# Cross attention 0 of a Perceiver kernel: key and value projections as three products of float16 halves, and x loaded first

## The reference

```python
def _mha_cross(x, mem, in_w, in_b, out_w, out_b):
    wq, wk, wv = (in_w[:D], in_w[D:2 * D], in_w[2 * D:])
    q = _split_heads(x @ wq.T + bq, H)
    k = _split_heads(mem @ wk.T + bk, H)
    v = _split_heads(mem @ wv.T + bv, H)
    scores = jnp.einsum('bhqd,bhkd->bhqk', q, k) * (1.0 / math.sqrt(hd))
    attn = jax.nn.softmax(scores, axis=-1)
    out = _merge_heads(jnp.einsum('bhqk,bhkd->bhqd', attn, v))
    return out @ out_w.T + out_b
x_self = _prob_sparse_self_attn(x, self_out_w, self_out_b)
x = _layernorm(x + x_self, ln1_g, ln1_b)
x_cross = _mha_cross(x, memory, cross_in_w, cross_in_b, cross_out_w, cross_out_b)
```

## Time and profile before

| what | value |
|---|---|
| time, median of 3 runs (all) | 3562.58 us (3560.48 to 3575.97) |
| the profiled execution | 3577.74 us, its span 3576.0 us |
| busy over the span | PE 93%, PEld 67%, DVE 70%, ACT 53%, POOL 31% |
| mean granted clock of TensorE | 0.958 of full speed |
| first instruction of TensorE | 23.0 us |
| cross attention 0 | 188.5 to about 1121 us |
| in it, from 300 to 1000 us: DVE's waits for maxima (L977) | 131.6 us |
| ACT's waits for scores (L998) there | 237.5 us |
| POOL's waits for evicted keys (L1173) and for queries (L1079) there | 327.6 and 100.7 us |
| 24 spread_keys DMAs on SP's queue, one batch | issued from 599.25 to 615.51 us, each landing 2.2 us after its issue |

### The profile page before, as it was taken

The page is one execution under the profiler, slowest core; times in us unless marked ns, Lnnn a source line. Parts: engine busy times, 40 slices in busy tenths (PEclk is TensorE's granted clock), DMA queues, the critical chain, the costliest instruction groups (busy, mean ns, idle before and its releaser), DMA issues. The chain is left out here.

```text
span 3576.0 us, 83011 instructions
## 1 busy us (share of the span) xinstructions
PE 3337.8 (93%) x32677; PEld 2384.9 (67%) x32913; DVE 2495.1 (70%) x7178; ACT 1909.3 (53%) x2964; POOL 1102.4 (31%) x795
## 2 busy tenths in 40 slices
PE   6879999999998888899999999999999999797999
PEld 4746666666666666677777777777777777565666
DVE  5657777777775444677777777777777777566544
ACT  4326666566665232566666666666666666444333
POOL 1033334333341001544434433444344333130000
PEclk9969999999999779999999999999999999897999
DMA  1023333333320010111111111111111110100000
GB/s 53 2 68 76 75 82 71 74 76 76 81 62 16 2 48 22 42 43 43 33 31 42 43 34 31 43 43 37 34 37 43 34 33 19 48 1 27 1 1 13
DMA packets 95125, 146.45 MB, mean 41 GB/s; under 512 B 14960, under 2 KB 72336, under 8 KB 93968
## 3 DMA queue, kind: packets, MB, share of 16 engines
q1 hardware_dynamic: 94736, 141.12, 14.7%
HBM read 100.66 MB, written 1.05 MB: 28 GB/s over the span
## 5 line engine op out<-in xcount | busy, mean ns | idle before, releaser
L2252 DVE SCALAR_TENSOR_TENSOR arena<-banks,arena 128x512 f16<-128x512 f32 (+1 forms) x1024 | 554.3, 583 | 308.7 <-ACT arena L2341 307.4
L2341 ACT ACTIVATE arena<-banks 128x512 f16<-128x512 f32 (+1 forms) x1024 | 471.3, 512 | 400.2 <-PE banks L2159 397.1
L1092 DVE TENSOR_REDUCE arena<-banks 128x1 f32<-128x512 f32 (+1 forms) x896 | 529.4, 627 | 186.7 <-PE banks L977 181.5
L1189 ACT ACTIVATE arena<-banks 128x1024 f32<-128x1024 f32 (+1 forms) x448 | 425.1, 964 | 315.3 <-PE banks L998 312.5
L2264 DVE CUSTOM_DVE_ANT_0 arena<-banks,arena 128x1024 f32<-128x1024 f32 (+1 forms) x512 | 494.3, 987 | 32.1 <-issue 31.9
L2348 ACT ACTIVATE arena<-arena 128x1601 f32<-128x1601 f32 x256 | 417.7, 1632 | 107.7 <-DVE arena L2270 105.7
L2159 PE MATMUL banks<-consts,arena 128*128 128x128 f32 (+1 forms) x3328 | 456.8, 275 | 7.1 <-DVE arena L2252 7.0
L2173 PE MATMUL banks<-arena 128*128 128x256 f16 (+1 forms) x1664 | 456.1, 274 | 0.7 <-ACT arena L2355 0.7
L2175 PE MATMUL banks<-arena 128*128 128x256 f16 (+1 forms) x1664 | 451.3, 271 | 0.0
L2174 PE MATMUL banks<-arena 128*128 128x256 f16 (+1 forms) x1664 | 450.3, 271 | 0.0
L2159 PEld LDWEIGHTS banks<-consts,arena 128*128 128x128 f32 (+1 forms) x3328 | 364.9, 141 | 17.2 <-issue 10.0
(11 more groups left out here) (360 smaller groups left out, 6141.2 us busy)
## 6 DMA issues: line engine op xcount, KB each, us to landing
arena<-in_ctxT SPq DMA_DIRECT2D x64, 800.5 KB, 4.5
arena<-arena SPq DMA_DIRECT2D x768, 50.0 KB, 2.2
arena<-in_ctx SPq DMA_DIRECT2D x32, 768.0 KB
arena<-in_mask SPq DMA_DIRECT2D x32, 200.1 KB, 4.6
arena<-in_m2w SPq DMA_DIRECT2D x3, 2048.0 KB, 8.3
arena<-in_xw SPq DMA_DIRECT2D x1, 2048.0 KB, 11.8
weights<-in_weights SPq DMA_DIRECT2D x1, 1920.0 KB, 7.8
arena<-in_ctx SPq DMA_DIRECT2D x32, 32.5 KB
```

The costliest lines, as they stand in the source:

```text
L1092: eng.tensor_reduce(o, s, AX, ALU.max).then_inc(a_max, 1)
L1189: eng.activation(pr[0:w, at % 4, :].rearrange("p (x n) -> p x n", x=2)[:, :, 0:n], c.ps[0:w, bank:bank + 2, 0:n], ACT.Exp, scale=scale).th ...
L2252: eng.scalar_tensor_tensor(out=part(ptl, g, gr), in0=turned(gr), scalar=TOP, in1=part(pth, g, gr), op0=ALU.mult, op1=ALU.subtract).then_in ...
L2341: eng.activation(part(pth, g, gr), turned(gr), ACT.Copy, scale=TOP).then_inc(t_high, 1)
```

## The change

- Context and the two weight matrices of the key and value projections are scaled into float16's range and split into a high and a low float16 half; each projection is the sum of three products (high x high, high x low, low x high). The first pair (i = 0) keeps the float32 projections.
- For the weights this is done once: `weights_peaks` and `weights_split` on VectorE, with `weights_row` on TensorE between them (a matmul with ones, through bank 7).
- For each further batch: `magnitudes` on ScalarE sums the absolute values of each context row of 1601 (128 partitions) after exps 5 of even units, `diagonal` on GpSimd spreads the sums on a diagonal, `ctx_row` on TensorE adds them over partitions (bank 7, after mix 6 of odd units), `ctx_scale` on VectorE makes the scale (reduce, floor, reciprocal, unit) after queries, and `split_ctx` on GpSimd scales and splits the context (three instructions, 128 x 1601) after split_queries. For batch (1, 0) ctx_row and ctx_scale stand in step 4 of the first unit, and magnitudes after its exps 0.
- The evictions of keys and values get a scale from memory; context loads wait for the split of the batch before in place of the projections.
- The loads are x in two halves, then consts, rows, weights, with semaphores of their own; the statistics and the normalisation of x alternate by group.

```diff
     def sp(eng):
+        x = A["x"].rearrange("(i b) l d -> (b l) i d", b=2)
+        eng.dma_start(c.x[:, 0:G, :], x[:, 0:G, :]).then_inc(c.x_loaded[0], 16)
+        eng.dma_start(c.x[:, G:PAIRS, :], x[:, G:PAIRS, :]).then_inc(c.x_loaded[1], 16)
+        eng.dma_start(c.c[:], A["consts"]).then_inc(c.consts_loaded, 16)
+        eng.dma_start(c.r[:], A["rows"]).then_inc(c.loaded, 16)
         eng.dma_start(c.w[:], A["weights"]).then_inc(c.loaded, 16)
-        eng.dma_start(c.r[:], A["rows"]).then_inc(c.loaded, 16)
-        eng.dma_start(c.c[:], A["consts"]).then_inc(c.loaded, 16)
-        eng.dma_start(c.x[:], A["x"].rearrange("(i b) l d -> (b l) i d", b=2)).then_inc(c.loaded, 16)
...
-    m.after = [(c.loaded, 64), (constant, 5)]
+    m.after = [(constant, 5)]
...
-        norms.dve_stats(eng, lambda i: c.x[:, i, :])
-        for g in range(GROUPS):
-            norms.dve_apply(eng, g, lambda i: c.x[:, i, :], lambda i: xn[:, i, :])
+        for g in range(GROUPS + 1):
+            if g < GROUPS:
+                if g < 2:
+                    eng.wait_ge(c.x_loaded[g], 16)
+                norms.dve_measure(eng, g, lambda i: c.x[:, i, :])
+            if g > 0:
+                norms.dve_apply(eng, g - 1, lambda i: c.x[:, i, :], lambda i: xn[:, i, :])
...
         def body(i, more):
-            if more:
-                load_ctx(i + 1, 0)
+            if i == 0 and more:
+                load_ctx(1, 0)
+            if i > 0 and more:
+                load_ctx(i + 1, 1)
             spread_keys(i, 1, 0)
             spread_keys(i, 1, 1)
+            if i == 0 and more:
+                load_ctx(1, 1)
+            if i + 2 < PAIRS:
+                load_ctx(i + 2, 0)
             if more:
-                load_ctx(i + 1, 1)
                 spread_keys(i + 1, 0, 0)
                 spread_keys(i + 1, 0, 1)
...
+        def diagonal(i, b):
+            n = batch_no(i, b)
+            eng.wait_ge(c_total, n + 1)
+            wait_if(eng, c_row, n)
+            eng.tensor_tensor(diag_c, c.C("ident"), total[:, b, :].to_broadcast([P, P]), ALU.mult).then_inc(c_diag, 1)
+
+        def split_ctx(i, b):
+            n = batch_no(i, b)
+            x = ctxT[:, b, :]
+            eng.wait_ge(c_inverse, n + 1)
+            eng.tensor_tensor(x, x, per_c[:, b, :].to_broadcast([P, S]), ALU.mult).then_inc(c_scaled, 1)
+            eng.wait_ge(c_scaled, n + 1)
+            if i > 1:
+                eng.wait_ge(v_ps, (i - 1) * 8 + 4 * b + 4)
+            eng.tensor_tensor(ch[:, b, 0:S], x, c.one[:].to_broadcast([P, S]), ALU.mult).then_inc(c_high, 1)
+            eng.wait_ge(c_high, n + 1)
+            eng.tensor_tensor(cl[:, b, 0:S], x, ch[:, b, 0:S], ALU.subtract).then_inc(c_split, 1)
...
         def body(i, more):
             if more:
-                for b in range(2):
-                    split_keys(i + 1, b)
-                    split_queries(i + 1, b)
+                split_keys(i + 1, 0)
+                diagonal(i + 1, 1)
+                split_queries(i + 1, 0)
+                split_ctx(i + 1, 1)
+                split_keys(i + 1, 1)
+                if i + 2 < PAIRS:
+                    diagonal(i + 2, 0)
+                split_queries(i + 1, 1)
+                if i + 2 < PAIRS:
+                    split_ctx(i + 2, 0)
...
+            eng.matmul(o, wh[:, 0, :], ch[:, b, a:z], start=True, stop=False)
+            eng.matmul(o, wh[:, 0, :], cl[:, b, a:z], start=False, stop=False)
+            eng.matmul(o, wl[:, 0, :], ch[:, b, a:z], start=False, stop=True).then_inc(k_ps, 1)
...
+                    eng.matmul(o, ch[:, b, r], wh[:, 1, :], start=True, stop=False)
+                    eng.matmul(o, ch[:, b, r], wl[:, 1, :], start=False, stop=False)
+                    mm = eng.matmul(o, cl[:, b, r], wh[:, 1, :], start=False, stop=True)
...
+        def ctx_row(i, b):
+            n = batch_no(i, b)
+            take_bank7((c_top, n + 1))
+            eng.wait_ge(c_diag, n + 1)
+            eng.matmul(c.ps[:, 7, 2 * P:3 * P], ones, diag_c, start=True, stop=True).then_inc(c_row, 1)
...
+                        elif more:
+                            ctx_row(1, 0)
                     elif st == 6 and v % 2 == 1 and more:
                         queries(i + 1, v // 2)
                     mix(i, v, st)
+                    if st == 6 and v == 1 and more:
+                        ctx_row(i + 1, 1)
+                    if st == 6 and v == 3 and i + 2 < PAIRS:
+                        ctx_row(i + 2, 0)
...
+        def ctx_scale(i, b):
+            n = batch_no(i, b)
+            eng.wait_ge(c_row, n + 1)
+            eng.tensor_reduce(top_c, c.ps[:, 7, 2 * P:3 * P], AX, ALU.max).then_inc(c_top, 1)
+            eng.wait_ge(c_top, n + 1)
+            eng.tensor_scalar(floor_c, top_c, 1e-25, 1 / TOP, ALU.max, ALU.mult).then_inc(c_floor, 1)
+            eng.wait_ge(c_floor, n + 1)
+            eng.reciprocal(per_c[:, b, :], floor_c).then_inc(c_inverse, 1)
+            if i > 1:
+                eng.wait_ge(v_made, (i - 1) * 8 + 4 * b + 4)
+            eng.tensor_scalar(units[:, b, :], per_top, floor_c[:, 0:1], None, ALU.mult).then_inc(c_units, 1)
...
+            eng.activation(o, ps, ACT.Identity, bias=c.W("c_bk"), scale=units[:, b, 0:1]).then_inc(k_copied, 1)
...
+                eng.activation(o, s, ACT.Identity, scale=units[0:w, b, 1:2]).then_inc(v_made, 1)
+
+        def magnitudes(i, b):
+
+            eng.wait_ge(ctx_loaded[b], i * 16 + 16)
+            if i > 1:
+                eng.wait_ge(v_ps, (i - 1) * 8 + 4 * b + 4)
+                eng.wait_ge(c_diag, batch_no(i - 1, b) + 1)
+            eng.activation(ch[:, b, 0:S], ctxT[:, b, :], ACT.Abs, accum_out=total[:, b, :]).then_inc(c_total, 1)
```

More of the change, by code:

```diff
@@ L808, in cross_attention_0 @@
     om, s1, rd = k.f32(4, L), k.f32(L), k.f32(L)
-    sem = lambda n: c.sem(f"x0_{n}")
+    ch, cl = k.f16(2, S + 1), k.f16(2, S + 1)
+    wh, wl = k.f16(2, D), k.f16(2, D)
+    ones, diag_w, diag_c = k.f32(P), k.f32(2, P), k.f32(P)
+    peak_w, top_w, per_top, to_f16 = (k.f32(2) for _ in range(4))
+    total, top_c, floor_c, per_c = k.f32(2, 1), k.f32(1), k.f32(1), k.f32(2, 1)
+    units = k.f32(2, 2)
+    TOP = 32768.0
+    sem = lambda n: c.sem(f"x0_{n}")
+    ones_set, w_peaks, w_diag, w_row, w_top, w_floor, w_inverse, w_high, w_low = (sem(f"w_{n}") for n in (
+        "ones", "peaks", "diag", "row_psum", "top", "floored", "inverse", "high", "low"))
+    c_total, c_diag, c_row, c_top, c_floor, c_inverse, c_units = (sem(f"ctx_{n}") for n in (
+        "total", "diag", "row_psum", "top", "floored", "inverse", "units"))
+    c_scaled, c_high, c_split = sem("ctx_scaled"), sem("ctx_high"), sem("ctx_split")
     two = lambda n: [sem(f"{n}{i}") for i in range(2)]
@@ L907, in pool @@
         split_queries(0, 1)
+        if PAIRS > 1:
+            diagonal(1, 0)
+            split_ctx(1, 0)
         def body(i, more):
             if more:
-                for b in range(2):
-                    split_keys(i + 1, b)
-                    split_queries(i + 1, b)
+                split_keys(i + 1, 0)
[8 more added lines that the diff above has]
+                    split_ctx(i + 2, 0)
         pairs(eng, body)
@@ L927, in keys @@
             take_bank7((k_copied, i * 8 + 4 * b + n + 1))
[L928 to L931 removed]
+            a, z = chunks[n]
+            o = c.ps[:, 7, 0:z - a]
+            if i == 0:
+                if n == 0:
+                    eng.wait_ge(ctx_loaded[b], 16)
+                eng.matmul(o, c.W("c_wk"), ctxT[:, b, a:z], start=True, stop=True).then_inc(k_ps, 1)
+                return
+            if n == 0:
+                eng.wait_ge(w_low, 2)
+                eng.wait_ge(c_split, batch_no(i, b) + 1)
+            eng.matmul(o, wh[:, 0, :], ch[:, b, a:z], start=True, stop=False)
+            eng.matmul(o, wh[:, 0, :], cl[:, b, a:z], start=False, stop=False)
+            eng.matmul(o, wl[:, 0, :], ch[:, b, a:z], start=False, stop=True).then_inc(k_ps, 1)
         def values(i, b, n):
@@ L1031, in pe @@
             keys(0, 1, n)
+        weights_row()
         for a in range(STEPS):
@@ L1127, in final, with weights_peaks, weights_split @@
             eng.tensor_tensor(c.o[r, i, b * L:(b + 1) * L], c.ps[r, 7, 0:L], rd[r, :], ALU.mult).then_inc(f_out, 1)
+        def weights_peaks():
+            for x, name in enumerate(("c_wk", "c_wv")):
+                eng.tensor_reduce(peak_w[:, x:x + 1], c.W(name), AX, ALU.max, apply_absolute_value=True).then_inc(w_peaks, 1)
+            for x in range(2):
+                eng.wait_ge(w_peaks, x + 1)
+                eng.tensor_scalar(diag_w[:, x, :], c.C("ident"), peak_w[:, x:x + 1], None, ALU.mult).then_inc(w_diag, 1)
+        def weights_split():
+            eng.wait_ge(w_row, 1)
+            eng.tensor_reduce(top_w, c.ps[:, 7, 0:2 * P].rearrange("p (w n) -> p w n", w=2), AX, ALU.max).then_inc(w_top, 1)
+            eng.wait_ge(w_top, 1)
+            eng.tensor_scalar(per_top, top_w, 1e-25, 1 / TOP, ALU.max, ALU.mult).then_inc(w_floor, 1)
```

(25 more changed lines are left out.)

39 lines of the change are left out of this document (32 added, 7 removed).

## The result

The changed kernel takes 3670.88 us (median of four runs, 3669.96 to 3671.22) beside 3566.24 us (3560.48 to 3575.97) for the kernel before in the same series: the ratio is 1.029, 95% interval 1.0271 to 1.0308. It is 104.6 us slower. The forecast was 3628 with a range to 3665, so the direction and the main mechanism (a VectorE instruction held behind GpSimd) were right and the size fell short, by 43 us against the forecast and by 6 against the range. The profiled execution took 3671.2 (span 3669.4). Two executions in what follows were in a slow state, 6316.28 us of the kernel before and 4196.51 us of a variant of experiment 6, and the ratios leave them out.

The account below looks back on a forecast made before the run. TensorE bounds steps 0 to 3 of each unit, VectorE steps 4 to 6. Values +74.2, keys -5.4, last values unit -1.2, entry +12, start -14: +65.6 on 3577.7 gives 3643.3, less 15.1 is 3628 us; range 3515 to 3665.

Parts of the forecast that it names:

- Projections: TensorE's float16 key and value chunks: 0.41 and 0.37 us less per full chunk; step 3 maxima of keys units 0.8 earlier.
- Keys unit: Unit projecting keys: its CAST waits for GpSimd's key split, leaving -0.18 us instead of -0.8.
- Values unit without the hold: VectorE's wait for ctx_row plus ctx_scale eats the saving; CAST at T + 9.65, T being the end of queries on VectorE.
- The hold: Values unit: spread_max's CAST waits until GpSimd's third context split instruction ends, +2.56 us in each of 29 units.
- Entry and start: Once each: entry into the stage +12 us (7 to 18); earlier start of TensorE -14 us (-11 to -15).
- that the clock stays up behind a 2.5 us wait: TensorE in values units: no clock loss priced after the wait; the low-clock row had 5.1 us of idle time.
- rival A: The main forecast: values units' CAST held by the third split, keys units nearly unchanged; 3628 us, chance 0.45.
- E: As rival A, and TensorE's clock falls after each wait for some 5 us: 29 x 2.5 more, 3700; chance 0.08.
- B: Values units' CAST waits under 0.3 us for the third split or gains 0.5: 3546 us; chance 0.20.
- C: CASTs of both units go free of GpSimd, or the hold does not occur: 3514 us; chance 0.15.
- D: Values units' CAST held, keys units' CAST free: 3604 us; chance 0.09.
- F: VectorE instructions with two SBUF inputs wait for GpSimd too, about 0.7 us per keys unit: 3649; chance 0.03.

Follow-up runs that it names:

- experiment 6: experiment 3's kernel without the context's maximum over partitions (diagonal, ctx_row, 128x128 reduce): 3586.61 us; with filler products on TensorE before shifts as well: 3539.76 us.
- experiment 3: Changed kernel with GpSimd's third context split instruction waiting until spread_max of its unit has ended: 3578.32 us, ratio 1.0037.
- Experiments 2: Kernel before plus three scratch 128x1601 GpSimd instructions per batch behind split_queries: 3709.86 us; with the third behind spread_max of the values unit: 3564.92 us.
- Experiment 5: Changed kernel with filler products on TensorE before shifts (18 in units with v even, 3 in the others): 3644.66 us, ratio 1.0215.
- experiment 1: spread_max's CAST replaced by a TENSOR_TENSOR times one: changed kernel 3671.79 us, kernel before 3567.84 us.
- experiment 4: Changed kernel with the third context split instruction made in two halves of 800 and 801 columns: 3663.76 us, ratio 1.0274.

## Why the forecast was right, and where it fell short

**Projections: right but for 0.2.** In the kernel of experiment 3, with neither a held CAST in the values unit nor (in most periods) a low clock, the way from the values unit's CAST to the keys unit's is 12.88 us (615.69 to 628.57) against 13.52 before (640.75 to 626.40 + 27.87). The forecast had 0.8 less; it is 0.64.

**Keys unit: right.** The hold by the key split took back 0.5 of it: keys CAST to T is 5.17 (628.57 to 633.74) against 4.65. The net is -0.12; the forecast was -0.18.

**Values unit without the hold: right.** The CAST came at T + 9.77 (forecast 9.65, before 9.70). The queue behind ctx_row and ctx_scale ate the saving; experiment 6 prices the part of ctx_row and the reduce at 0.67.

**The hold: right in place and size.** T + 9.26, 9.39 forecast, for the third split's start; T + 12.31, 12.44 forecast, for the CAST's end. It added (2.54 + 2.79) / 2 - 0.18 = 2.49 us per values unit; the forecast was 2.56. Experiments 2 and 3 show it by taking it away and by making it alone.

**Entry and start: right.** T of the first pair's first batch fell from 267.12 to 264.87, 2.25 us earlier. The start gave 13.8 of this (23.05 to 9.25, forecast 14), so the entry cost 11.5 (forecast 12). Where one ends and the other begins is not sharp: at the stage's first queries this execution was 15.6 us ahead (189.25 against 204.90), and it lost 13.4 from there. The two largest pieces are TensorE's wait before the first maxima, behind weights_split on VectorE (5.07, where it was 0.78 before; forecast 4 more), and its wait for the first context split (4.30, forecast 6), with a low clock behind it:

```profile
215.13 1.20 PE L1068 MATMUL banks<-arena 64*128 64x512 bf16 x2 [5.07 <-DVE arena L1190]
...
250.87 0.59 PE L1003 MATMUL banks<-arena 128*128 128x512 f16 x1 [4.30 <-POOL arena L955]
```

**The step that failed: that the clock stays up behind a 2.5 us wait.** The forecast took rival A at 0.45 and gave E, the same with a falling clock, 0.08, since the only row of a low clock had 5.1 us of idle time before it. E was what happened. The period without the clock's share would be 27.81 + 2.49 = 30.30 (forecast 30.25); it was 31.45, so the clock and its consequences cost 1.15 us per period, 29 x 1.15 = 33 us. E had the length of the low stretch right on average (4.9 us per batch, 5 forecast), but its price of 2.5 for it was twice too high: a batch lost 1.15. That steps in which VectorE sets the pace lose little by a low clock would explain it and was not tried. Experiment 5 gives 26 of the 33 us back, with 51 us of low clock left of 143. One row with a long idle time bounds the time from above only; it says nothing of shorter waits, and I read it as if it did.

**The sum, checked.** In the profiled executions the last CAST of the stage moved from 1109.59 to 1209.06, +99.5, where the forecast's terms give +65.6; the 33.9 between are about the clock's 33. The rest of the program took 2466.4 before and 2460.3 after, 6 less. The second step that failed is small: I carried the 15.1 us by which the profiled execution of before lay above its median over to the new kernel. At least part of it was in this execution alone, since the rest of the program took 2452 to 2463 us in the other profiles, and the profiled execution of after lies at its own median. So 3643.3 + 33.9 - 6.1 = 3671.1 (measured 3671.2), and the median 3670.9 has nothing to be taken off. Of the 43 us by which the forecast was short 34 are thus the clock's and 9 this second step's (15.1 less 6.1).

**Rivals.** B and C needed the CAST to find GpSimd idle; that did not occur by itself, and where it was arranged for the values unit (experiment 3) the time was 3578, not 3546 or 3514. Most periods there took 27.81, where B has about 27.4, since the keys CAST was held for 0.6 of its 0.8 us, and the longer ones add 8 us to the stage; with 11 for the first that is 19 of the 32 us to B, and the rest is open. D did not occur: in the changed kernel the keys CASTs took 0.24 to 0.60 instead of 0.18. F's mechanism is real (experiments 1 and 4), against what I read from the earlier trace rows. Its price does not show as a line of its own: in the changed kernel the CAST comes first and is held, and the next finds GpSimd between two instructions or idle.

## What to carry to other kernels

When a step is moved to GpSimd, line up its instructions with the short SBUF instructions in VectorE's critical chain: the cost is not GpSimd's busy time but the rest of whichever long instruction is running when a short one comes, and one wait in GpSimd's queue (here 93 us of 105) can take it away. Where TensorE waits for another engine in every period, price the clock as a term of its own, also for waits of half a microsecond that lie close together, and look whether harmless work can stand in the gap. Less work alone need not be less time: experiment 6 had less work than experiment 3, its shortest period was shorter, and it was slower, because the clock fell more often (22 low stretches against 7 in 29 periods).

## What was not expected of the hardware

The hold is not bound to one form: a TENSOR_TENSOR of 128x4 with two SBUF inputs took 2.54 us, as the CAST did, instead of 0.17 (experiment 1), and 1.51 as the second in a row (experiment 4), while a TENSOR_REDUCE from SBUF took its usual 0.17 us inside GpSimd's third split (620.60 in the changed kernel), as did the 128x1 TENSOR_SCALAR during split_queries (611.93, 0.15, while GpSimd's L931 ran from 611.79 to 612.40).

TensorE's clock fell behind 2.29 us of idle time (with 0.33 and 0.21 soon after), in 29 of 29 batches, and in experiment 6 behind three stretches of 0.43, 0.20 and 0.21 us; 0.43 us of products put into the first of them kept it up (1.00 instead of 0.93 over 300 us). What exactly decides between the two levels was not tried and stays open; in the kernel of experiment 3 most periods with the same short waits (0.43, 0.20, 0.21) kept the higher level.
